# Folded query projection of two token halves on two column halves of the array, and rotations as two wide products

## The reference

```python
q_hk = (hidden_q @ Wq.T).reshape(Bv, Sv, H, K)
q_big = jnp.einsum('bshk,hkq->bshq', q_hk, w_kc_q)
q_big = _apply_rope(q_big, sin_q[None, :, None, :], cos_q[None, :, None, :])
...
q_r = jnp.einsum('bshq,hqr->bhsr', q_big, W_qr)
k_r = jnp.einsum('bld,hdr->bhlr', kv_r, W_kr)
scores = jnp.einsum('bhsr,bhlr->bhsl', q_r, k_r)
```

## Time and profile before

| | |
|---|---|
| median of 3 runs | 1550.45 us (1539.77 to 1553.62) |
| the profiled execution: span, first to last instruction | 1563.7 us |
| ST_XA in it: first instruction of its matmul work to the barrier's end | 278.68 to 442.04 us |
| layer norm stage ahead of it (ST_N2): last vector result | 273.62 us |

### The profile page before, as it was taken

The page is one execution under the profiler, slowest core; times in us unless marked ns, Lnnn a source line. Parts: engine busy times, 40 slices in busy tenths (PEclk is TensorE's granted clock), DMA queues, the critical chain, the costliest instruction groups (busy, mean ns, idle before and its releaser), DMA issues. The chain is left out here.

```text
span 1563.7 us, 21601 instructions
## 1 busy us (share of the span) xinstructions
PE 1450.8 (93%) x7635; PEld 1100.7 (70%) x7635; DVE 935.0 (60%) x1619; ACT 630.5 (40%) x1151; POOL 789.6 (50%) x621
## 2 busy tenths in 40 slices
PE   7788999899989999999999998988999998899998
PEld 4455566566646676676766755567988887899998
DVE  2752112466686768767686753577878774444554
ACT  2432221344423434424244342456666653333333
POOL 3732002367647769768677673057565551233332
PEclk9998999799999899989989999999999999999999
DMA  8014113510011101011010000101010001443441
GB/s 306 1 44 142 34 38 86 179 53 24 1 39 57 58 0 58 1 58 58 1 57 7 14 1 14 71 28 33 23 55 1 28 1 42 120 119 120 121 121 52
DMA packets 60321, 88.66 MB, mean 57 GB/s; under 512 B 7556, under 2 KB 44612, under 8 KB 60230
## 3 DMA queue, kind: packets, MB, share of 16 engines
q1 hardware_dynamic: 59206, 85.82, 17.2%
q0 software_dynamic: 1024, 1.64, 0.4%
HBM read 81.92 MB, written 5.41 MB: 56 GB/s over the span
## 5 line engine op out<-in xcount | busy, mean ns | idle before, releaser
L1007 ACT ACTIVATE prob<-PS 121x800 f32<-121x800 f32 x192 | 158.1, 837 | 254.0 <-PE PS L2041 238.3
L1405 DVE TENSOR_REDUCE mx<-PS 128x1 f32<-128x482 f32 (+1 forms) x312 | 186.7, 649 | 56.6 <-PE PS L2019 54.6
L622 POOL TENSOR_TENSOR e_wl<-e_wf,e_wh 128x768 fp32r<-128x768 f32 x33 | 71.0, 2151 | 174.4 <-ACT e_wh L905 152.6
L717 POOL TENSOR_TENSOR hT<-hT,prob 121x800 f32<-121x800 f32 x56 | 109.7, 1958 | 71.1 <-ACT prob L1007 68.9
L2018 PE MATMUL PS<-kth,qs 128*128 128x482 f32 (+1 forms) x312 | 131.5, 422 | 13.7 <-DVE mx L1405 10.3
L2056 PE MATMUL PS<-prob,kvn 121*64 121x400 f32 (+1 forms) x768 | 136.1, 503 | 0.9 <-ACT prob L1007 0.9
L717 POOL TENSOR_TENSOR xc<-xc,prob 121x800 f32<-121x800 f32 x56 | 114.8, 2050 | 30.3 <-ACT prob L1007 25.8
L2019 PE MATMUL PS<-kl,qm 66*128 66x482 f32 (+1 forms) x312 | 125.4, 402 | 0.0
L2038 PE MATMUL PS<-qs,kth 128*121 128x400 f32 (+1 forms) x384 | 113.1, 377 | 3.1 <-ACT prob L1007 2.4
L2041 PE MATMUL PS<-qm,kl 66*121 66x400 f32 (+1 forms) x384 | 105.4, 357 | 0.0
L2056 PEld LDWEIGHTS PS<-prob,kvn 121*64 121x64 f32 (+1 forms) x768 | 52.3, 137 | 71.2 <-issue 69.0
(11 more groups left out here) (301 smaller groups left out, 3650.1 us busy)
## 6 DMA issues: line engine op xcount, KB each, us to landing
e_wb<-routing SPq DMA_DIRECT2D x32, 400.0 KB, 3.9
wgu<-in_L_ffn_gate_up_proj SPq DMA_DIRECT2D x8, 1024.0 KB, 14.3
krt<-in_ctx_T SPq DMA_DIRECT2D x8, 722.0 KB, 4.1
ksw<-in_ctx_Tswap SPq DMA_DIRECT2D x8, 722.0 KB, 5.8
wdn<-in_L_ffn_down_proj SPq DMA_DIRECT2D x8, 512.0 KB, 7.9
wq<-in_L_ffn_Wq SPq DMA_DIRECT2D x4, 1024.0 KB, 5.3
wo<-in_L_ffn_Wo SPq DMA_DIRECT2D x4, 1024.0 KB, 5.7
e_wf<-in_L_ffn_Wg SPq DMA_DIRECT2D x32, 128.0 KB, 2.2
```

What stands on the lines that cost most here:

```text
L622: pool.tensor_tensor(m["wl"][:, slot], m["wf"][:, slot], m["wh"][:, slot].bitcast(fp32), ALU.subtract).then_inc(ms["wlo"], 1)
L717: pool.tensor_tensor(acc, acc, prob[:, n % RING], ALU.add).then_inc(xb["ap"], 1)
L1007: act.activation(prob[0:k, n % RING], PS[0:k, 2 * (n % 2):2 * (n % 2) + 2, 0:GC], ACT.Exp).then_inc(xb["ex"], 1)
L1405: dve.tensor_reduce(mx3[:, m, g:g + 1], PS[:, 4 + k % 3, 0:SEG[g][1]], AX.X, ALU.max).then_inc(xb["free"], 1)
```

## The change

The fold is kept once (`wkrT` and `wp` lose their second copy). The final is made once per head instead of once per step: both token halves go through it in one go, half 0 to partitions 0 to 63 of bank 6 and half 1 to partitions 64 to 127, which are two column halves of the array. It moves from one step behind qb to two steps behind it. The four products of a rotation become two of 96 x 800 that read two banks at once (the order of `ropeq` changes for that); GpSimd subtracts and adds in place, in a ring of four tiles (`xc`, `hT`, `sq` and a new `rp3`). With bank 7 free, qh alternates between banks 0 and 7. ScalarE's and VectorE's splitting of the result is written once per head: ScalarE three copies (`high_heads`), VectorE two subtractions (`low_parts`), some of them from one half of the partitions to the other. The fold of a head is made at the end of its own second step, not one head ahead. On the SP queue the query weights of the first group go first, then its fold weights, the tables, and the second group.

```diff
-            for n in range(4):
-                sp.dma_start(ropeq[:, n, :], a["rope_q"][n]).then_inc(xa["rope"], 16)
...
-            for t in range(2):
-                load_folds(t)
-                load_queries(t)
+            load_queries(0)
+            load_folds(0)
+            for n in range(4):
+                sp.dma_start(ropeq[:, n, :], a["rope_q"][n]).then_inc(xa["rope"], 16)
+            load_queries(1)
+            load_folds(1)
             end_stage(sp, ST_N2)
...
             for u in range(2 * H1):
-                pool.wait_ge(xa["rp"], 4 * u + 4)
-                if u >= 2:
-                    pool.wait_ge(xa["qp"], u - 1)
-                pool.tensor_tensor(rr[u % 2][:, 0], rp[u % 2][:, 0], rp[u % 2][:, 1], ALU.subtract).then_inc(xa["rr"], 1)
-                pool.tensor_tensor(rr[u % 2][:, 1], rp[u % 2][:, 2], rp[u % 2][:, 3], ALU.add).then_inc(xa["rr"], 1)
+                pool.wait_ge(xa["rp"], 2 * u + 2)
+                r = rp[u % 4]
+                pool.tensor_tensor(r[:, 0], r[:, 0], r[:, 3], ALU.subtract).then_inc(xa["rr"], 1)
+                pool.tensor_tensor(r[:, 1], r[:, 1], r[:, 2], ALU.add).then_inc(xa["rr"], 1)
...
+            def high_heads(h):
+
+                act.wait_ge(xa["qp"], h + 1)
+                lo, hi = (PS[r, 6, 0:HALF].rearrange("p (b s) -> p b s", s=S) for r in (slice(0, DC), slice(DC, P)))
+                act.activation(qs[0:DC, 0:HB, h, :], lo, ACT.Copy).then_inc(xa["qlo"], 1)
+                if h >= 1:
+                    act.wait_ge(xa["qst"], 2 * h)
+                act.activation(qlo[DC:P], PS[DC:P, 6, 0:HALF], ACT.Copy).then_inc(xa["qlo"], 1)
+                act.activation(qs[0:DC, HB:B, h, :], hi, ACT.Copy).then_inc(xa["qhi"], 1)
+            for s in range(2 * H1 + 4):
+                if s % 2 and s >= 5:
+                    high_heads((s - 5) // 2)
...
+            def rotate_heads(u):
+
+                dve.wait_ge(xa["qb"], u + 1)
+                if u >= 4:
+                    dve.wait_ge(xa["qp"], u // 2 - 1)
+                bl = 2 + 2 * (u % 2)
+                both = PS[0:QH, bl:bl + 2, 0:HALF].rearrange("p k (b s) -> p k b s", s=S)
+                o = rp[u % 4].rearrange("p k (b s) -> p k b s", s=S)
+                dve.tensor_tensor(o[:, 0:2], both, cosq, ALU.mult).then_inc(xa["rp"], 1)
+                dve.tensor_tensor(o[:, 2:4], both, sinq, ALU.mult).then_inc(xa["rp"], 1)
...
-                    if s >= 1:
-                        pe.wait_ge(xa["ql"], XP + s)
+                    if s >= 2:
+                        pe.wait_ge(xa["ql"], XP + s - 1)
...
-                u = s - 2
-                if s >= 2 * H1:
-                    keep_busy(0, 6)
-                if u >= 0:
-                    pe.wait_ge(xa["rr"], 2 * u + 2)
...
-                        last = mm(PS[:, 6 + u % 2, 0:HALF], wp[:, u // 2, c, :], rr[u % 2][:, c], start=(c == 0), stop=(c == 1))
+                if s > 2 * H1:
+                    keep_busy(0, 10)
+                if s % 2 == 0 and s >= 4:
+                    h = (s - 4) // 2
+                    pe.wait_ge(xa["rr"], 4 * h + 4)
...
+                        for q in range(2):
+                            last = mm(PS[q * DC:(q + 1) * DC, 6, 0:HALF], wp[:, h, c, :], rp[(2 * h + q) % 4][:, c],
+                                      start=(c == 0), stop=(c == 1))
                     last.then_inc(xa["qp"], 1)
-                if s % 2 == 0 and s // 2 + 1 < H1:
-                    fold(s // 2 + 1)
+                if s % 2 and s < 2 * H1:
+                    fold(s // 2)
```

More of the change, by code:

```diff
@@ L196, in flamingo @@
         wqlo = sb("wqlo", [P, 2, NC, P], fp32r, stack=st2)
-        rp = [t_[0:QH].rearrange("p c (k n) -> p (c k) n", k=2) for t_ in (xc, hT)]
-        rr = [sq[0:QH, c].rearrange("p (k n) -> p k n", k=2) for c in range(2)]
+        rp3 = sb("rp3", [P, NC, T], stack=st2)
+        rp = [t_[0:QH].rearrange("p c (k n) -> p (c k) n", k=2) for t_ in (xc, hT, sq, rp3)]
         st2.close()
@@ L966, in _ @@
                         act.wait_ge(xa["qb"], s - 1)
[L967 to L970, removed]
-                if u >= 0:
[L972 to L977, removed]
+                    act.activation(qkh[:, s % 2], PS[:, 7 * (s % 2), 0:HALF], ACT.Copy).then_inc(xa["qhe"], 1)
+                    if s % 2:
+                        if s // 2 + 2 < H1:
+                            high_projection(s // 2 + 2)
+                        keep_fold(s // 2)
+                        if s >= 3 and s // 2 + 1 < H1:
+                            high_latent(s // 2 + 1)
             end_stage(act, ST_XA)
@@ L1355, in slices @@
                             low_act(m, ms, n - 1, (k - 1) % 8)
-            cosl, sinl, cosh, sinh = (ropeq[:, n, None, :].to_broadcast([QH, HB, S]) for n in range(4))
+            cosq, sinq = (ropeq[:, n:n + 2, None, :].to_broadcast([QH, 2, HB, S]) for n in (0, 2))
             dve.wait_ge(xa["rope"], 64)
@@ L1362, in low_heads @@
                     dve.wait_ge(xa["qb"], s - 1)
-                dve.tensor_tensor(qkl[:, s % 2], PS[:, 0, 0:HALF], qkh[:, s % 2].bitcast(fp32), ALU.subtract).then_inc(xa["ql"], 1)
+                dve.tensor_tensor(qkl[:, s % 2], PS[:, 7 * (s % 2), 0:HALF], qkh[:, s % 2].bitcast(fp32), ALU.subtract).then_inc(xa["ql"], 1)
             for q in range(2):
@@ L1390, in _ @@
+            for s in range(2 * H1 + 4):
+                if s < 2 * H1:
+                    low_heads(s)
+                if s % 2 and s >= 5:
+                    low_parts((s - 5) // 2)
+                if 0 <= s - 1 < 2 * H1:
+                    rotate_heads(s - 1)
             end_stage(dve, ST_XA)
@@ L1945, in fold @@
                 for c in range(2):
-                    mm(PS[0:QH, 1, c * P:(c + 1) * P], wqrT[:, j, i, c, :], wkrT[:, j, i].rearrange("p a d -> p (a d)"),
-                       start=True, stop=True)
+                    mm(PS[0:QH, 1, c * DC:(c + 1) * DC], wqrT[:, j, i, c, :], wkrT[:, j, i], start=True, stop=True)
                 half_ = slice(DC * (h % 8 // 4), DC * (h % 8 // 4) + DC)
                 mm(PS[half_, 1, 2 * P:2 * P + D], kckv[:, j, i], wohT[:, j, i], start=True, stop=True).then_inc(xa["f"], 1)
-            fold(0)
-            for s in range(2 * H1 + 2):
+            for s in range(2 * H1 + 3):
                 if s < 2 * H1:
                     h, q = s // 2, s % 2
-                    if s >= 1:
-                        pe.wait_ge(xa["ql"], XP + s)
+                    if s >= 2:
+                        pe.wait_ge(xa["ql"], XP + s - 1)
                     if s < 2:
```

68 lines of the change are left out of this document (23 added, 45 removed).

## The result

The changed kernel takes 1505.58 us (median of five executions, 1503.47 to 1526.64) where the kernel before takes 1550.45 in the same series; the ratio is 0.973, with an interval of 0.9694 to 0.9766. The forecast was 1511.5 with a range of 1499 to 1530. The profiled execution of the changed kernel happens to be the longest of the five, with a span of 1524.9 us.

What follows compares the result with a forecast made beforehand. TensorE's own list and its wait for GpSimd were taken to bound the stage ST_XA. Heads 29.8 plus start 10 minus end 0.4 gave 39 us, so 1550.45 - 39 = 1511.5 us, range 1499 to 1530.

Steps and rivals of the forecast that it cites:

- The finals on two column halves: TensorE's finals in ST_XA: eight half-height matmuls take 1.39 us instead of 2.9, gaining 1.5 a head, less 0.2 for ends.
- Rival (b): Finals in ST_XA: the halves do not overlap, finals stay at 2.9 us, a head 8.7, time 1532; chance 0.06.
- The wait for GpSimd: TensorE's wait for GpSimd's addition before each final: 0.8 us a head goes, with 1.2 us to spare.
- What is late next: ScalarE's three copies delay VectorE's `qkl` and the next qb: covered by 1.7 us, else each missing microsecond paid 16 times.
- VectorE's wide products: VectorE's rotation in ST_XA: each product of 800 columns takes 0.95 us, between 0.9 and 1.1.
- The 14 heads: Middle of ST_XA, step 2 to step 30: a head falls from 9.33 to 7.2 us, gaining 29.8 us.
- Rival (d): VectorE's wide products run at half rate, over 2.2 us, and set an 11.1 us head: 1567 us, slower; chance 0.03.
- The start: Loads and first steps through step 2: 10 us gained, 4.3 from an earlier qh; bounds 3 and 12.
- The end: Behind the last qb of ST_XA: 8.5 us instead of 8.1, a cost of 0.4 us.
- (a): ST_XA's chain of copies and additions becomes the bound, GpSimd keeping 1.5 us of waiting a head: 1526 us; chance 0.2.
- (c): ST_XA: no second fall of the clock and a head of 6.8 us, gaining 47 us: 1503; chance 0.12.
- main case: Whole kernel: heads, start and end together gain 39 us, giving 1511.5 us; chance 0.58.

Runs made afterwards that it cites:

- that run: Changed kernel with each fold moved directly ahead of a final, plus twelve empty matmuls around the barrier before the stage: 1504.89 us, ratio 0.9692.

## Why the prediction was right, and where it missed

**The finals on two column halves: right.** I put the eight instructions at 1.39 us and their ends at 0.2. The block takes 1.49 us with one end in it, and parting the halves costs 1.64 us a head: 1.33 for four passes that no longer run beside others, 0.31 for a second pair of ends. Rival (b), that the halves do not overlap, is refuted, but its price was good: 8.7 us and 1532 forecast, 8.96 and 1531 measured with the halves apart. The Trainium skill, "TensorEngine Tiling (Array Packing)", section "Tiling Modes", says that a switch of the tiling mode drains the array. The trace agrees: two switches cost 0.31 us a head, which is the worst case that I had weighed, 0.16 a switch, and not the 0.2 that I put into the sum. The block as a whole was priced nearly right all the same, 1.39 and 0.2 against 1.33 and 0.31.

**The wait for GpSimd: right.** 12.6 us became 0.3. I counted 1.2 us to spare; in the head above GpSimd's sum ends at 340.34 + 1.04 = 341.38 and the final starts at 343.34, 1.96 to spare. That it is the second step that buys this is shown by the kernel without it, which is slower than before.

**What is late next: right.** I saw ScalarE's copies covered by 1.7 us. The `qkl` that hangs on them ends at 347.63; the qb that needs it follows the qh of 348.29, 1.2 us later: 1.86 to spare. What I did not see is how that queue closes into a ring with GpSimd when the cover goes; I priced the loss at each missing microsecond paid 16 times, and it was far more.

**VectorE's wide products: the price right, the worth nil.** 0.98 us reported and 0.91 from start to start, against 0.95. Rival (d) is refuted. Four narrow ones give the same time.

**The 14 heads: mechanism right, the term too large by 3.2 us.** 29.8 forecast, 26.6 measured. Two things make the difference. First, the head is 7.32 and not 7.2. I took 1.1 us for each qh and qb, from the one that has its like on both sides; in the new list each stands next to a fold or to finals at one end, and the four are 1.19, 1.17, 1.21 and 1.20, 0.37 in all above my 4.4. The fold came out 0.08 below, and the block's ends, counted by me apart, are partly these same gaps. 14 x 0.12 = 1.7 us. Second, the first of the 14 heads lasts 8.77, 1.45 more than the rest, but only by VectorE's marks. TensorE's own head there is 7.33 us (289.69 to 297.02). VectorE's last product stands 0.05 us behind that qh at the first mark and 1.49 behind the next one at the second (298.51), where the two low parts have come into its list. So this 1.45 is no lost time; the marks put it into the start.

**The start: the term too small, beyond its bound.** 10 us forecast with bounds of 3 and 12, 15.4 measured, 14.0 without the 1.45 just named. Two steps failed. "The tables then land ... and VectorE waits for them ahead of its first subtraction": it did not. Its subtraction at 276.93 names a wait for ScalarE's `hh` and none for the tables, and qh came 278.02 - 264.95 = 13.07 us after the first load instead of 280.82 - 262.52 = 18.30: 5.2 us won, not 4.3. And "I count the last product of step 2 at about 293", 16.5 us after a qh at 276.5; it took 289.74 - 278.02 = 11.72. I had left the clock low for much of that time; it was low for 3.4 us. The runs divide the 15.4: the loads alone bring 9.6 on the old list and 5.4 on the new one, and the new list alone, with the old loads, 40.2 - 30.2 = 10.0. Each of the two does away with one of the long low spells. The two gains are no sum: 9.6 and 10.0 by themselves, 15.4 together.

**The end: right.** -0.4 forecast, -0.3 measured.

**Rivals (a) and (c).** (a), the chain of copies and additions as the bound, is refuted as it stands: GpSimd is 0.88 us a head short of being it, though the kernel with more work for it shows that this is all the room. Nor did the emptying of the banks bind: TensorE's one wait in the stage after its first qh is the 0.3 us for GpSimd. The time, 1505.6, lies between the main case's 1511.5 and (c)'s 1503. Half of (c) came true, the clock that does not fall a second time, and its head of 6.8 did not. So the forecast came near because two errors, -3.2 in the heads and +5.4 at the start, partly cancel (-1.7 and +4.0 where the 1.45 is counted with the heads): 39 forecast, 41.7 in the stretch. The 3 us to the medians lie in other stages, within their spread. The mechanism was right; that the time came so near is in part luck.

## What to carry to other kernels

Two matmuls of 64 output rows that stand in one block on different column halves cost as much as one (1.49 us for both finals, 1.48 for one), and each such block costs 0.31 us for its two ends, so gather them into one. But a joint step waits for the later of its inputs: move it far enough back in the list before counting the gain, and follow for each engine in the ring what stands behind the instruction that waits. Where a stage starts, ask for the operands in the order in which they are needed first, and look at the granted clock in the next 20 us: the idle gap costs once as idle time and again as slow matmuls (here, the kernel before with the new loads had its qh only 2.65 us sooner, but 9.6 us won at the end of the start, with 3.4 us at the low clock in place of 17). An engine's fewer, wider instructions are worth nothing while it waits anyway.

## What was not expected of the hardware

The overlap of the column halves does not hang on the order of issue within a block: with both matmuls of one half ahead of both of the other, the first of the second half started 0.01 us behind the first of the first (338.53 and 338.54), and the block took the same 1.5 us. Nor need the two halves do the same work: the fold's 128 x 64 product with 256 columns and a final of 96 x 64 with 400 columns started at the same 327.25. Matmuls on different halves can even overtake each other: in a later head of that run `rp`'s final, issued behind `sq`'s, started at 334.24 and `sq`'s at 334.71, behind the fold's product on its own half. ScalarE's copy, which waits for the last one issued (`rp`), still began at 336.27, after the last pass of `sq` too.
